# A gated recurrence scanned one pipeline step behind its entry instead of two, with its TensorE products moved to the end of the step

## The reference

```python
x = x + _L0_attn_a_ref(_layernorm(x, axis=-1), ...)
x = x + _L0_ffn_ref(_layernorm(x, axis=-1), ...)      # experts, first time
x = x + _L0_attn_b_ref(_layernorm(x, axis=-1), ...)   # the recurrence
x = x + _L0_ffn_ref(_layernorm(x, axis=-1), ...)      # experts, second time

# the recurrence, for each batch:
k = jnp.einsum('btd,dh->bth', x, Wz) + bz
log_coeffs = -jax.nn.softplus(k)
log_values = -jax.nn.softplus(-k) + _log_g(jnp.einsum('btd,dh->bth', x, Wh) + bh)
a_star = jnp.cumsum(log_coeffs, axis=1)
h = jnp.exp(a_star + jax.lax.cumlogsumexp(log_values - a_star, axis=1))
out = layernorm of h over the 128 features, * gamma + beta, + x
```

## Time and profile before

| what | value |
|---|---|
| median of 3 runs (lowest, highest) | 1426.38 us (1421.06, 1432.44) |
| span of the profiled execution | 1524.2 us |
| busy in the whole span: PE, DVE, ACT, POOL | 1216.6, 1144.1, 967.7, 991.9 us |
| first and last start of the shifts in the recurrence | 979.8, 1210.0 us |
| mean granted TensorE clock, whole span | 0.890 |

### The profile page before, as it was taken

One profiled execution on the slowest core, in us unless ns is written; L12 is line 12 of the kernel. 1 busy time (PEld: TensorE's weight loads), 2 busy tenths in 40 slices (PEclk: granted clock), 3 DMA queues, 4 the chain that ended last, 5 costly groups with the idle time before them and its releaser, 6 DMA issues. The chain is left out here.

```text
span 1524.2 us, 38116 instructions
## 1 busy us (share of the span) xinstructions
PE 1216.6 (80%) x11689; PEld 1017.3 (67%) x11689; DVE 1144.1 (75%) x3833; ACT 967.7 (63%) x2078; POOL 991.9 (65%) x1131
## 2 busy tenths in 40 slices
PE   5889999999999999973788888577787449888850
PEld 3667777777777777753788888455566348788850
DVE  5489999999999999965566665488888546666638
ACT  3588888888888888851555544277777435455420
POOL 4346688888888888777355665237777835666530
PEclk9699999999999999995799997588878669999955
DMA  7211111111111111123222222112222122222228
GB/s 199 86 46 46 48 60 60 60 60 60 59 60 60 60 60 60 39 93 83 73 86 86 81 85 68 49 49 83 73 83 69 45 68 84 86 84 84 77 83 277
DMA packets 99443, 117.19 MB, mean 77 GB/s; under 512 B 17784, under 2 KB 79792, under 8 KB 99248
## 3 DMA queue, kind: packets, MB, share of 16 engines
q1 hardware_dynamic: 70560, 73.57, 16.3%
q0 software_dynamic: 16896, 35.16, 6.8%
q10 hardware_dynamic: 11792, 6.05, 1.4%
HBM read 47.56 MB, written 41.51 MB: 58 GB/s over the span
## 5 line engine op out<-in xcount | busy, mean ns | idle before, releaser
L1153 DVE TENSOR_TENSOR ebuf<-score_banks,region 128x768 f32<-128x768 f32 x256 | 243.6, 951 | 18.8 <-PE score_banks L862 13.1
L1402 ACT ACTIVATE region<-ebuf 128x768 f32<-128x768 f32 x256 | 215.9, 860 | 23.0 <-DVE ebuf L1153 23.0
L1380 ACT CAST copied<-max_banks 128x768 bf16<-128x768 f32 x251 | 201.9, 804 | 15.1 <-PE max_banks L850 12.5
L1842 POOL DMA_INDIRECT choice_rows<-second_yo,second_xg x136 | 133.1, 979 | 112.7 <-PE second_by L1880 69.3
L1842 POOL DMA_INDIRECT choice_rows<-first_yo,first_xg x136 | 130.7, 961 | 114.0 <-PE first_by L1880 65.9
L1694 POOL DMA_INDIRECT expert_rows<-d_rows,a_d_index x112 | 129.4, 1155 | 27.9 <-issue 17.2
L1918 ACT ACTIVATE second_silu<-second_bgu,second_biases 128x256 f32<-128x256 f32 (+1 forms) x144 | 61.0, 466 | 114.3 <-PE second_bgu L1871 66.7
L1918 ACT ACTIVATE first_silu<-first_bgu,first_biases 128x256 f32<-128x256 f32 (+1 forms) x144 | 61.9, 462 | 111.8 <-issue 83.6
L1954 DVE SCALAR_TENSOR_TENSOR second_hT<-second_bgu,second_biases,second_silu 128x256 f32<-128x256 f32 (+1 forms) x144 | 62.1, 464 | 70.3 <-ACT second_silu L1918 37.6
L905 PE MATMUL bankO<-region,vaug 128*32 128x256 f32 (+1 forms) x2048 | 111.1, 334 | 1.9 <-ACT region L1402 1.9
L853 PE MATMUL max_banks<-region_r 32*128 32x256 f32 x502 | 98.3, 388 | 11.9 <-DVE ebuf L1153 7.4
(11 more groups left out here) (369 smaller groups left out, 4531.6 us busy)
## 6 DMA issues: line engine op xcount, KB each, us to landing
region_r<-region_r SPq DMA_DIRECT2D x192, 128.0 KB
first_xg<-expert_rows SPq DMA_DIRECT2D x64, 132.0 KB
second_xg<-expert_rows SPq DMA_DIRECT2D x64, 132.0 KB
z_rows<-choice_rows SPq DMA_DIRECT2D x32, 256.0 KB
c_rows<-choice_rows SPq DMA_DIRECT2D x16, 512.0 KB
out<-xres ACTq DMA_DIRECT2D x16, 256.0 KB
choice_rows<-first_yo,first_xg POOLq DMA_INDIRECT x136
choice_rows<-second_yo,second_xg POOLq DMA_INDIRECT x136
```

The source lines that it names most:

```text
L1153: nc.vector.tensor_tensor(ebuf[:, half_of_ebuf(c, j), :, :], score_banks[:, :, 0:BK], bias32[:, plain(j), :], ALU.add).then_inc(scores_fre ...
L1380: nc.scalar.copy(copied[:, 2 * j:2 * j + 2, :], banks_of_max(c, j)[:, :, 0:BK]).then_inc(maxed_free, 1)
L1402: nc.scalar.activation(p32[:, j % 4, :, :], ebuf[:, half_of_ebuf(c, j), :, :], ACT.Exp).then_inc(exped, 1)
L1842: pool.indirect_dma_start(choice_dram, bass.IndirectOffsetOnAxis(ap=xg[:, i % G, t, E:E + 1].bitcast(I32), axis=0), yo[:, i % 4, t, :], No ...
```

## The change

A batch is scanned one step after its entry instead of two, and everything that follows (its end, the sending, the choosing and the placing) comes one step earlier too, so there are 38 steps. On VectorE the scan moves ahead of the shifts. On TensorE `back` moves from the front of the step to its end. No instruction is added to the work of a batch and none is taken away; step 38 carries no work of its own now, and one root, its shifts and its aggregation fall away.

```diff
-        LAST = B + 7
+        LAST = B + 6
         def scans(i):
+            return 1 <= i <= B
+
+        def ends(i):
             return 2 <= i <= B + 1
-        def ends(i):
+        def sends(i):
             return 3 <= i <= B + 2
-        def sends(i):
-            return 4 <= i <= B + 3
...
                     if ends(i):
-                        dve.wait_ge(h_full, i - 2)
+                        dve.wait_ge(h_full, i - 1)
...
                     if scans(i):
-                        valued = values(i - 2, q)
+                        valued = values(i - 1, 1 - q)
+                    if scans(i):
+                        scan(i - 1, 1 - q, valued)
                     if norms(i):
                         shifts(i, q)
-                    if scans(i):
-                        scan(i - 2, q, valued)
...
                     if ends(i):
-                        finish(i - 3, 1 - q)
+                        finish(i - 2, q)
...
-                    if scans(i):
-                        back(i - 2, q)
                     if enters(i):
                         turn_input(i, q)
                     if sends(i):
-                        turn(i - 4)
+                        turn(i - 3)
                     if enters(i):
                         gates_of(i, q)
                     if sends(i):
-                        router(i - 4, ranked)
+                        router(i - 3, ranked)
+                    if scans(i):
+                        back(i - 1, 1 - q)
```

More of the change, by code:

```diff
@@ L2115, in scans, with placed_in @@
         def scans(i):
+            return 1 <= i <= B
+        def ends(i):
             return 2 <= i <= B + 1
-        def ends(i):
+        def sends(i):
             return 3 <= i <= B + 2
-        def sends(i):
-            return 4 <= i <= B + 3
         def norms(i):
-            return i <= B + 3
+            return i <= B + 2
         def chosen_in(i):
+            return (i - 5) // 2 if i % 2 == 1 and 5 <= i <= B + 3 else None
+        def placed_in(i):
             return (i - 6) // 2 if i % 2 == 0 and 6 <= i <= B + 4 else None
-        def placed_in(i):
-            return (i - 7) // 2 if i % 2 == 1 and 7 <= i <= B + 5 else None
         def second_labels(m):
@@ L2139, in means_free @@
             if sends(i - 2):
-                engine.wait_ge(d_copied, i - 5)
+                engine.wait_ge(d_copied, i - 4)
             elif i >= 2:
@@ L2162, in statistics @@
                     if sends(i):
-                        dve.wait_ge(done, i - 3)
+                        dve.wait_ge(done, i - 2)
                         for t in range(2):
-                            ch.mark(nc.vector.bn_stats(stats[:, q, 4 + t, :], tile(i - 4, t)))
+                            ch.mark(nc.vector.bn_stats(stats[:, q, 4 + t, :], tile(i - 3, t)))
                     if enters(i):
@@ L2170, in statistics @@
                     if ends(i):
-                        dve.wait_ge(h_full, i - 2)
+                        dve.wait_ge(h_full, i - 1)
                         for t in range(2):
-                            ch.mark(nc.vector.bn_stats(stats[:, q, 2 + t, :], bh[1 - q][:, t * P:(t + 1) * P]))
+                            ch.mark(nc.vector.bn_stats(stats[:, q, 2 + t, :], bh[q][:, t * P:(t + 1) * P]))
                     ch.wait(ch.base + ch.n)
@@ L2271, in _ @@
                         nc.gpsimd.tensor_tensor(rs[:, q, :], arg[:, q, :], half[:], ALU.pow).then_inc(rooted, 1)
-                    if i >= 8 and q == 0 and not d.late((i - 8) // 2):
-                        scatter((i - 8) // 2, 1)
+                    if i >= 7 and q == 1 and not d.late((i - 7) // 2):
+                        scatter((i - 7) // 2, 1)
                     if placed_in(i) is not None:
@@ L2430, in _ @@
                     if sends(i - 1):
-                        take_logits(i - 5)
+                        take_logits(i - 4)
                     if gated(i):
@@ L2434, in _ @@
                     if ends(i):
-                        norm_outputs(i - 3, 1 - q, i)
+                        norm_outputs(i - 2, q, i)
                     if enters(i):
@@ L2438, in _ @@
                     if sends(i):
-                        apply(i - 4, i)
+                        apply(i - 3, i)
                     if enters(i):
@@ L2442, in _ @@
                     if sends(i):
-                        take(i - 4)
-                        copy(i - 4, i)
+                        take(i - 3)
+                        copy(i - 3, i)
                 act.wait_ge(known, 1)
```

## The result

The changed kernel takes 1562.8 us (median of 6 runs, 1557.6 to 1564.8) against 1426.9 us (median of 6 runs of the kernel before): 1.095 times as long, 95% interval 1.091 to 1.098. The forecast was 1557, in a range of 1490 to 1595. The profiled execution after has a span of 1555.9 us.

What follows compares the result with a forecast made beforehand. The prediction took a chain through several engines to bound the kernel. Full loops of 11.3 us and shorter end intervals gave 369.8 us against 230.2; the 139.6 more, times 0.936, is 131: 1426 + 131 = 1557 us, range 1490 to 1595.

Steps and rivals of the forecast that it cites:

- The loop: In the recurrence, every link between two shifts becomes serial: 9.16 us at 2.4 GHz, 12.09 at 1.2 GHz, against 6.58.
- the residual products: TensorE's six products into the residual bank in `back`, a link of 2.76 us at 1.2 GHz, 1.30 at 2.4 GHz.
- gate products and router: TensorE's link from the first gate product to the router's end: 2.73 us at 1.2 GHz, 1.48 at 2.4 GHz.
- shifts to gate products: The link from VectorE's shifts to TensorE's first gate product, with both ScalarE normalisations in it: 2.43 us.
- the slow sum: All links of one recurrence step added up with TensorE at 1.2 GHz: 12.09 us.
- The mixed case: TensorE at half clock at each step's head, lifted near its end: 11.3 us a loop, 1557 us, chance 0.65.
- The full-clock rival: The serial loop at 2.4 GHz throughout: 9.16 us a full loop, 1492 us in all, chance 0.15.
- The sum: The 34 intervals between first and last shifts take 369.8 us together against 230.2, 139.6 us more in the trace.
- The scale: Trace gains and losses times 0.936, the runs' median over the profiled span, turning 139.6 us into 131.
- no engine is full: In 160 us of the steady part VectorE is busy 138, TensorE 127, ScalarE and GpSimd 125; a chain sets the step.
- The wait's size: VectorE idle some 3 us in each step before the statistics of the transposes, ended by TensorE.
- The scan ahead of the shifts: On VectorE, it costs 0.9 us a step, not 1.52, because GpSimd's root of 1.54 us runs beside.

Runs made afterwards that it cites:

- e4: The changed kernel with eight unread products added in each step, ahead of TensorE's input transpose: 1486.7 us.
- the second profile: The kernel before, unchanged, profiled once more; its span is that of the timed runs, and its shifts take 230.0 us from first to last.
- e10: The kernel before with a second, unread root of 128x6 values on GpSimd in each step: 1469.0 us.
- e7: The kernel before with unread products, four in odd steps and one in even ones, in TensorE's wait for the scan: 1430.0 us.
- e5: The changed kernel with VectorE's swap alone undone, the shifts ahead of the scan again: 1535.5 us.
- e2: The kernel before with `back` moved to the end of TensorE's step, depth and VectorE's order unchanged: 1543.5 us.
- e1: The changed kernel with `back` at the front of TensorE's step again, all else as changed: 1430.2 us.
- e8: The changed kernel with `back` at the front of TensorE's step and the shifts ahead of values and scan on VectorE: 1429.1 us.
- e3: The changed kernel with the six residual products moved to the front of TensorE's step, transposes and centred products still last: 1472.9 us.

## Why the prediction was right, and where it was not

**The loop.** It held link by link. The order of the rows, the wait that moved to L2173 and the wait before L2284 (141.4 us, 13.5 of it the first step's; about 4 in each of the others, as forecast) stand in the trace. In the step shown, of the terms at 1.2 GHz, the residual products (2.76), the transposes (0.42 against 0.43, estimated), the statistics (1.29 against 1.28) and values with scan (1.52) came out as summed; gate products and router were 2.57 instead of 2.73, shifts to gate products 2.35 instead of 2.43, placing 0.82 instead of 0.94. It is 11.73 long where the slow sum was 12.09.

**The clock.** The mixed case was the right one: 11.20 a loop against 11.3, steps between 10.5 and 12.1, and a granted clock of 0.72, just above the 0.6 to 0.7 forecast. That the loop came out so close is in part luck. The prediction took half of what residual products and transposes save at full clock, which leaves 2.35 us for them; on average over the 29 loops they took 2.61. Gate products and router (2.62 on average), shifts to gate products (2.35) and placing (0.82) were 0.3 shorter together than their terms, and the two misses cancel. The full-clock rival is what e4 shows when TensorE is kept busy; its sum was 0.3 too high. The Trainium skill ("TensorE: Matmul & The Clock Gate", Part 1, The HAM clock gate) calls the slow clock the default that activity releases. The trace agrees: 0.72 with TensorE idle once a step, 1.00 in e4 with most of the idle time filled (its wait before L2284 is 35.1 us in all, 141.4 without the added products).

**The sum.** Forecast 139.6 us more between first and last shifts; measured 138.5. The 29 full loops took 324.9 us (forecast 327.7), the first three intervals 28.1 (26.7), the last two 15.7 (15.4).

**The scale: wrong.** The prediction multiplied by 0.936 because the profiled execution was 97.8 us longer than the runs. That assumed the excess to lie everywhere. It lay in the two expert stages: the first experts' products (L1869) ran from 732.9 to 964.4 us there, and from 732.3 to 913.3 in the second profile, while the shifts took 230.2 and 230.0; that stage took 50 us longer, the second experts 42. Unscaled, the sum gives 1426 + 140 = 1566, and 1562.8 was measured. Both are in range, and the step was still a wrong one: a ratio of whole executions says nothing on one stage.

**What bounds the kernel now: wrong.** The prediction read "no engine is full" from busy times of 125 to 138 us in 160, and so took a chain through TensorE for the bound. GpSimd's busy time leaves out the gap of about 0.3 us behind each scatter; with it the queue is full in the second profile and nearly full in the first. e10 shows that GpSimd sets the steady step, and the profiles at three clocks (e7) that TensorE's clock does not. Two smaller claims fall with it: the price of TensorE's wait for the scan was indeed nothing, but because of GpSimd; and a step taken away saves some 6.6 us only where nothing is lost elsewhere (e5 against e2: 6.7; e1 and e8: no gain).

**The wait's size.** 5.2 us in each step before L2173, where the prediction said some 3. The rows of the kernel before would have given it: VectorE is busy 138 of 160 us, 5.9 us of a step of some 6.8, which leaves 5.4 of a loop of 11.3. The chain doesn't depend on it.

**The scan ahead of the shifts.** Put at 0.9 us a step; e5 gives 27 us over 29 loops, 0.9, of which the scan itself is 0.7 and the rest mostly the clock, so the agreement is luck. Undoing TensorE's order alone (e1) wins back 133 of the 136 us, undoing VectorE's alone 27; the parts don't add, since with the products in front (e1) depth and scan together cost some 5 us.

## What to carry to other kernels

In a software pipeline of in-order engines, a product that is moved to the end of its step and is needed by another engine at the start of the next one closes a loop of everything between; count the steps of slack between producer and consumer on each edge before moving either. A wait that shows on one engine (33 us on TensorE here) is worth nothing when another's queue is full, and fullness has to be read with the gaps of its issues, not from busy time. Work that needs no late result (the residual products) belongs in the idle time, where it shortened the chain and raised the clock a little as well (e3).

## What the runs showed of the hardware that was not expected

- Eight useless products a step raised the granted clock from 0.72 to 1.00 and made the changed kernel 76 us faster. In the kernel before, whose step hangs on GpSimd, executions with 0.84 and with 0.95 in the steady part had the same time there (230.2 and 230.0 us).
- The granted clock of one kernel's steady part differs between executions: 0.84 in the first profile of the kernel before, 0.95 in the same part of the second, and 1.00 in 110 us of that:

```profile
968.00:1128.00 160.00, 110.13 (x624) 86.19 (x623) 139.34 (x763) 123.05 (x355) 132.22 (x118) 0.95 0.26 77
985.00:1095.00 110.00, 70.55 (x430) 55.64 (x430) 95.74 (x528) 83.58 (x242) 91.79 (x80) 1.00 0.27 80
```

- One profiled execution of the kernel before was 98 us longer than the next, 50 us of it in the first expert stage and 42 in the second (first to last product of L1869). What slowed it there stays open.
